# Graph layer on one NeuronCore: the ring of gathered rows and edge weights grows from eight places to twelve, and VectorE builds the weights before it adds the sums

## The chip, the cores and the metric

The kernel runs on one core of one Trainium2 chip. The metric is the device time of one execution in microseconds (us). Three runs of the kernel before took 794.12, 795.60 and 796.25 us, a median of 795.6 us.

## The reference

3125 nodes have 256 features each, and 50000 edges carry a source, a destination (sorted) and one of eight relations. Cut to the part that the change touches:

```python
xn = _layernorm(x)
W = jnp.einsum('rb,bio->rio', comp, basis)         # 8 relations out of 4 bases
h_all = jnp.einsum('ni,rio->nro', xn, W)
msgs = h_all[src, edge_types]
agg = jax.ops.segment_sum(msgs, dst, num_segments=3125)
h = gelu(agg + xn @ loop_w + h_bias + xn)          # then a layer norm
x = x + layer_norm(h) + mix(xn)                    # mix: attention without positions
x = x + ffn(_layernorm(x))                         # 32 experts, one for each node by argmax
```

The kernel turns the sum around: for each base it first sums the source rows by destination, weighted by the edge's factor for that base, and multiplies by the bases afterwards.

## The kernel before, in words

**The work.** The edges lie in 392 tiles of 128 edges. Eight tiles are an octet (49 octets, `q`), two tiles a quarter (PE's `edges(q, quarter)`), four a half. For each tile GpSimd (POOL) gathers 128 rows of `xn_d` into one place of `gath` (line 534), VectorE (DVE) builds `wmat`, which for each edge holds its four base weights at the column of its destination within a window of 36 nodes (lines 1152 and 1162, one build for each half), and TensorE (PE) multiplies gathered rows by weights (line 786). The products of a quarter stand in one PSUM bank of four; DVE adds them into `acc` at an address that it reads from a table (`add_edges`, line 1189, two adds for each quarter `w`).

**What runs beside.** `edge_schedule` writes the order by hand. Octets 0 to 6 ("max") also take the largest key of each column: PE's `key_max` (line 793) in each quarter, DVE's `reduce_max` (line 1197) after each half; the third quarter's `key_max` waits for the reduction that follows the first half. Octets 7 to 19 ("sum") compute keys (lines 800 and 801), ScalarE (ACT) their exponentials (line 621), and PE the weighted sums (line 805). Octets 20 to 22 are three small steps. Octets 23 to 48 ("chain") each finish one tile of 128 nodes: PE's `early` (817) and `product` (828), ACT's gelu, DVE's `first_stats`, `second_stats` and `finish_row` (line 1234 is its last step), PE's `turn_row` (line 840) in the third quarter, which waits for `finish_row`, and `logits` (850). After the edges comes a tail with the 32 experts.

**The ring.** `gath` and `wmat` have eight places, one for each tile of an octet. POOL's gather of tile `n` waits until tile `n - 8` was multiplied (semaphore `multiplied`, which starts at 8). DVE adds the quarter's sums, builds `hit` between the two quarters of a half, and builds the weights of the same half of the next octet at the end, when all tiles of this half are multiplied:

```python
def add_edges(q, half, bases):
    for w in range(half * OCT // PAIR // 2, (half + 1) * OCT // PAIR // 2):
        v.wait_ge(multiplied, OCT * q + PAIR * (w + 1) + OCT)
        ...
        if w % 2 == 0:
            build_hit(q + 1, half)
    build_weights(q + 1, half)
```

**The tail.** After the last octet POOL gathers 25 tiles of rows ordered by expert (line 559), PE turns them (1015) and multiplies them by the experts' weights (`hidden`, line 1025), and ACT copies and activates (718 and 729).

Of the kernel before, what the change touches and what calls it, by code (L numbers as in the profile page):

```python
# [22 lines left out]
P = 128  # L23
N, D, E = 3125, 256, 50000
R, B, X, H = 8, 4, 32, 64
KD = D // P
NT = -(-N // P)
LAST = N - (NT - 1) * P
NPAD = NT * P
WIN = 36  # L30
PAIR = 2
OCT = 8
NOCT = -(-E // (P * OCT))
# [69 lines left out]
def gps_layer(nc, x, src_t, type_rows, dst_t, dst_rows, basis, comp, loop_w, h_bias, ln_gamma, ln_beta,  # L103
              w_qk, b_qk, w_v, b_v, bn_gamma, bn_beta, router_w, router_b, w1_t, b1_t, w2_t, relation_of,
              group_mask, out):
    with ExitStack() as ctx:
        def sb(name, shape, dt=F32):
            return ctx.enter_context(nc.sbuf_tensor(name, shape, dt))
# [18 lines left out]
        gath = sb("gath", [P, OCT, D])  # L127
        wmat = sb("wmat", [P, OCT, B, WIN])
        hit = sb("hit", [P, OCT // 2, WIN])
# [123 lines left out]
        gathered = [sem(f"gathered{k}") for k in range(OCT)]  # L253
# [67 lines left out]
        f_in = [sem(f"f_in{s}") for s in range(NT)]  # L321
# [174 lines left out]
        def _(pool):  # L496
# [34 lines left out]
            def octet(q, beside, i):  # L531
                for k in range(OCT):
                    pool.wait_ge(multiplied, OCT * q + k + 1)
                    g.indirect_dma_start(gath[:, k, :], None, xn_d,  # L534
                                         bass.IndirectOffsetOnAxis(ap=src_i[:, OCT * q + k:OCT * q + k + 1], axis=0)).then_inc(gathered[k], 16)
# [21 lines left out]
            for t in range(NT):  # L557
                n = rows(t)
                g.indirect_dma_start(token[0:n, t, 0:2 * D], None, rows_d,  # L559
                                     bass.IndirectOffsetOnAxis(ap=inv_i[0:n, t:t + 1], axis=0)).then_inc(f_in[t], 16)  # L560
# [176 lines left out]
        def _(pe):  # L737
# [38 lines left out]
            def edges(q, quarter):  # L776
                if quarter % 2 == 0:
                    pe.wait_ge(wmat_built, 2 * q + quarter // 2 + 1)
                pair = range(PAIR * quarter, PAIR * quarter + PAIR)

                pe.wait_ge(added, KD * (4 * q + quarter + 1))
                for m in range(KD):
                    for k in pair:
                        if m == 0:
                            pe.wait_ge(gathered[k], 16 * q + 16)
                        ins = t_.matmul(ps_edge[quarter][:, m * B * WIN:(m + 1) * B * WIN], gath[:, k, m * P:(m + 1) * P],  # L786
                                        wmat[:, k, :, :].rearrange("p b w -> p (b w)"), start=k == pair[0], stop=k == pair[-1])
                        if m == KD - 1:
                            ins.then_inc(multiplied, 1)
# [196 lines left out]
            def rank_and_experts():  # L986
# [90 lines left out]
        def _(v):  # L1077
# [68 lines left out]
            def build_hit(q, half):  # L1146
# [4 lines left out]
                v.wait_ge(wmat_built, n) if not isinstance(q, int) or n > 0 else None  # L1151
                d.tensor_tensor(hit[:, :, :], rel[:, cut].unsqueeze(2).to_broadcast([P, w, WIN]),
                                iota[:, 0:WIN].unsqueeze(1).to_broadcast([P, w, WIN]), ALU.is_equal).then_inc(hit_built, 1)

            def build_weights(q, half):
                w = OCT // 2
                n = 2 * q + half
                cut = ds(OCT * q + half * w, w) if not isinstance(q, int) else slice(OCT * q + half * w, OCT * q + half * w + w)
# [3 lines left out]
                d.tensor_tensor(wmat[:, half * w:half * w + w, :, :], hit[:, :, :].unsqueeze(2).to_broadcast([P, w, B, WIN]),  # L1162
                                wts[:, :, cut].rearrange("p b t -> p t b").unsqueeze(3).to_broadcast([P, w, B, WIN]),
                                ALU.mult).then_inc(wmat_built, 1)

            for half in range(2):
                build_hit(0, half)
                build_weights(0, half)
# [212 lines left out]
            def rank_and_experts(o):  # L1381
# [87 lines left out]
                def finish(t):  # L1469
                    n = rows(t)  # L1470
                    place = f_ys[0:n, t * D:(t + 1) * D]
                    v.wait_ge(f_in[t], 16)
# [109 lines left out]
```

## Time and profile before

| | |
|---|---|
| median of 3 runs | 795.6 us (794.12 to 796.25) |
| the profiled execution's own time | 790.61 us |
| its span, first to last instruction | 788.7 us |
| mean granted TensorE clock | 0.886 |
| busy: PE, POOL, DVE, ACT | 585.8, 458.2, 386.3, 163.5 us |
| first edge product to the last | 53.3 to 631 us |

Busy time says how long an engine executed, not what set the pace. "Idle before" is the time in which an engine stood still before an instruction, and the name behind it is who ended that. "remote" is a signal whose sender the profile could not match. A matmul's end in these rows is modelled, not observed.

### The profile page before, as it was taken

Reading aid. Unit: us, or ns where it says so; the run is one execution under the profiler, and the core shown is the slowest. Engines: PE = TensorE matmul, PEld = TensorE weight load, DVE = VectorE, ACT = ScalarE, POOL = GpSimd, SP = SyncE. Lnnn points to the kernel's source line nnn. Section 1 sums busy time; section 2 is a strip of 40 time slices with the busy share of each in tenths; the row PEclk is TensorE's granted clock in tenths of the full one; section 3 lists DMA queues with packets and bytes.
Section 4 is the critical chain, followed back from the end, with each engine's and each line's share of the span. In section 5 each row is a group of like instructions: output and inputs, shape, how many; then the busy total and the mean of one; then the engine's idle time right before and its main releaser. Section 6 shows DMA issues by size and latency. Waiting matters only on the chain.

```text
span 788.7 us, 10440 instructions
## 1 busy us (share of the span) xinstructions
PE 585.8 (74%) x3181; PEld 471.6 (60%) x3181; DVE 386.3 (49%) x1272; ACT 163.5 (21%) x345; POOL 458.2 (58%) x464
## 2 busy tenths in 40 slices
PE   0366686888888768698999798897979982419980
PEld 0356675666665647477777666775858741318860
DVE  2844445333322334446666646456547677303552
ACT  0450000000000001022332312132122350115520
POOL 9146676666666666566676667666666400740165
PEclk9969999898999998699999888899989995559986
DMA  8563333333333344234434433334334326640021
GB/s 227 157 185 88 87 99 88 90 89 91 93 91 94 91 141 121 68 94 126 123 115 131 126 112 115 103 114 128 110 108 130 108 99 166 200 126 2 15 81 72
DMA packets 41872, 86.78 MB, mean 110 GB/s; under 512 B 11280, under 2 KB 23378, under 8 KB 41491
## 3 DMA queue, kind: packets, MB, share of 16 engines
q0 software_dynamic: 22576, 61.01, 26.7%
q1 hardware_dynamic: 18372, 22.95, 9.4%
q10 hardware_dynamic: 864, 2.08, 1.1%
q8 instruction: 29, 0.48, 0.2%
q14 instruction: 31, 0.25, 0.1%
HBM read 73.21 MB, written 12.80 MB: 109 GB/s over the span
## 4 chain that ended last, share of the span: by engine, by line
PE 56%; another core or an unknown queue 14%; DVE 10%; issue 7%; DMA 4%; POOL 3%; ACT 2%; SPq 1%; DVEq 0%; ACTq 0%; POOLq 0%
PE ps L786 23%; PE ps L828 11%; PE ps L817 6%; PE ps L1025 3%; PE ps L1034 2%; PE ps L793 2%; DMA both<-in_x 2%; PE ps L800 2%; POOL gath L534 2%; PE ps L805 2%; DMA gath<-xn_d,src_i 1%; POOL out L564 1%; PE ps L850 1%; PE ps L840 1%
## 5 line engine op out<-in xcount | busy, mean ns | idle before, releaser
L534 POOL DMA_INDIRECT gath<-xn_d,src_i x392 | 386.5, 986 | 214.9 <-issue 90.9
L786 PE MATMUL ps<-wmat,gath 128*128 128x144 f32 x1568 | 257.8, 309 | 25.5 <-DMA gath<-xn_d,src_i 10.7
L786 PEld LDWEIGHTS ps<-wmat,gath 128*128 128x128 f32 x1568 | 229.4, 203 | 50.8 <-issue 22.4
L1189 DVE TENSOR_TENSOR acc_raw<-acc_raw,ps 128x144 f32 x392 | 101.8, 300 | 283.2 <-PE ps L786 203.5
L1162 DVE TENSOR_TENSOR wmat<-hit,wts 128x576 f32<-128x576 f32 x100 | 75.3, 753 | 0.3
L564 POOL DMA_INDIRECT out<-acc_raw,inv_i x25 | 25.4, 1015 | 55.5 <-DVE acc_raw L1473 49.1
L1482 DVE SCALAR_TENSOR_TENSOR acc_raw<-ps,wts,acc_raw 128x256 f32 x56 | 27.0, 482 | 59.7 <-PE ps L1034 46.6
L559 POOL DMA_INDIRECT both<-rows_d,inv_i x25 | 24.3, 971 | 52.6 <-DVE inv_i L1436 45.2
L828 PE MATMUL ps<-wk_et,acc_raw 128*128 128x256 f32 (+1 forms) x200 | 53.1, 391 | 0.0
L828 PE MATMUL ps<-wq_wv,acc_raw 128*128 128x256 f32 (+1 forms) x200 | 52.6, 388 | 0.0
L817 PE MATMUL ps<-cmat,both 128*128 128x512 f32 (+1 forms) x100 | 52.5, 651 | 0.0
L1025 PE MATMUL ps<-acc_raw,gath 128*64 x224 | 33.3, 308 | 24.9 <-ACT acc_raw L718 22.7
L1025 PEld LDWEIGHTS ps<-acc_raw,gath 128*64 128x64 f32 x224 | 28.8, 156 | 30.7 <-issue 30.7
L793 PE MATMUL ps<-both,wk_et 128*128 128x256 f32 (+1 forms) x104 | 29.9, 414 | 18.4 <-DVE top L1197 18.4
L828 PEld LDWEIGHTS ps<-wq_wv,acc_raw 128*128 128x128 f32 (+1 forms) x200 | 36.9, 193 | 4.8 <-issue 0.2
L805 PE MATMUL ps<-both,wk_et 128*128 128x257 f32 (+1 forms) x100 | 28.5, 410 | 14.8 <-ACT wk_et L621 7.8
L828 PEld LDWEIGHTS ps<-wk_et,acc_raw 128*128 128x128 f32 (+1 forms) x200 | 35.1, 194 | 3.6 <-issue 0.2
L621 ACT ACTIVATE wk_et<-ps 128x256 f32<-128x256 f32 x24 | 9.2, 384 | 126.9 <-remote 71.3
L840 PE MATMUL ps<-ident,both 128*128 128x128 f32 (+1 forms) x50 | 11.2, 308 | 31.4 <-issue 16.4
L750 PE MATMUL ps<-ident,both 128*128 128x128 f32 x50 | 10.8, 387 | 31.6 <-DVEq L1116 23.7
L793 PEld LDWEIGHTS ps<-both,wk_et 128*128 128x128 f32 x104 | 19.6, 210 | 21.8 <-DVE top L1197 19.6
L646 ACT ACT_TABLE_LOAD x25 | 32.1, 1283 | 0.5
(194 smaller groups left out, 619.7 us busy)
## 6 DMA issues: line engine op xcount, KB each, us to landing
gath<-xn_d,src_i POOLq DMA_INDIRECT x392
rows_d<-both SPq DMA_DIRECT2D x24, 256.0 KB
both<-in_x SPq DMA_DIRECT2D x24, 128.0 KB
both<-in_x SPq DMA_DIRECT2D x4, 640.0 KB, 17.2
xn_d<-both SPq DMA_DIRECT2D x4, 640.0 KB
acc_raw<-in_w_t SPq DMA_DIRECT2D x1, 2080.0 KB
acc_raw<-in_w_t SPq DMA_DIRECT2D x1, 2048.0 KB, 7.5
acc_raw<-in_type_rows ACTq DMA_DIRECT2D x1, 1600.0 KB, 15.6
```

What stands on the lines that cost most here:

```text
L534: g.indirect_dma_start(gath[:, k, :], None, xn_d, bass.IndirectOffsetOnAxis(ap=src_i[:, OCT * q + k:OCT * q + k + 1], axis=0)).then_inc(ga ...
L564: g.indirect_dma_start(out, bass.IndirectOffsetOnAxis(ap=inv_i[0:n, t:t + 1], axis=0), f_ys[0:n, t * D:(t + 1) * D], None).then_inc(f_stor ...
L646: s.activation(h[0:n, t % 2, :], ps_mix[t % 2][0:n, 0:D], ACT.Gelu).then_inc(c.gelu_done, 1)
L786: ins = t_.matmul(ps_edge[quarter][:, m * B * WIN:(m + 1) * B * WIN], gath[:, k, m * P:(m + 1) * P], wmat[:, k, :, :].rearrange("p b w -> ...
L793: ins = t_.matmul(ps_mix[m][:, 0:n], wk[:, k, m * P:(m + 1) * P], xnt[:, k, ds(first, n)], start=k == 0, stop=k == KD - 1)
L805: ins = t_.matmul(ps_sum[m][:, 0:D + 1], et[0:n, j, m * P:(m + 1) * P], tile, start=start, stop=stop)
L817: t_.matmul(bank, xnt[:, k, P * t:P * t + n], cmat[:, k, :], start=k == 0, stop=False)
L828: ins = t_.matmul(ps_mix[t % 2][0:n, 0:D], acc[:, f, t * P:t * P + n], basis_sb[m][:, b, :], start=False, stop=f == KD * B - 1, skip_group ...
L1025: ins = t_.matmul(ps[4 + g % 2][0:H, f * P:(f + 1) * P], f_w[:, g % 2, f, k * H:(k + 1) * H], xts[:, ds(tiles[f] * D + k * P, P)], start=k ...
L1162: d.tensor_tensor(wmat[:, half * w:half * w + w, :, :], hit[:, :, :].unsqueeze(2).to_broadcast([P, w, B, WIN]), wts[:, :, cut].rearrange(" ...
L1189: d.tensor_tensor(place, place, ps_edge[w][:, m * B * WIN:(m + 1) * B * WIN].rearrange("p (b w) -> p b w", w=WIN), ALU.add).then_inc(added, 1)
L1482: d.scalar_tensor_tensor(place, ps[g % 2 * 2 + f // 2][:, f % 2 * D:(f % 2 + 1) * D], limit[:, p:p + 1], place, ALU.min, ALU.max).then_inc ...
```

## The change

`gath` and `wmat` now have `SLOTS = 12` places, three halves of four. Tile `n` uses place `n % 12`. The gather of tile `n` waits for the product of tile `n - 12`. The weights of half `2q + half + 2` are built at the start of `add_edges(q, half)`, ahead of its adds, and wait for the products of half `2q + half - 1`. Besides, in the tail two tiles share one `f_in` semaphore, so PE and DVE wait for two gathers where they waited for one.

```diff
+HALF = OCT // 2
+SLOTS = 3 * HALF
-        gath = sb("gath", [P, OCT, D])
-        wmat = sb("wmat", [P, OCT, B, WIN])
-        hit = sb("hit", [P, OCT // 2, WIN])
+        gath = sb("gath", [P, SLOTS, D])
+        wmat = sb("wmat", [P, SLOTS, B, WIN])
+        hit = sb("hit", [P, HALF, WIN])
...
-                for k in range(OCT):
-                    pool.wait_ge(multiplied, OCT * q + k + 1)
-                    g.indirect_dma_start(gath[:, k, :], None, xn_d,
-                                         bass.IndirectOffsetOnAxis(ap=src_i[:, OCT * q + k:OCT * q + k + 1], axis=0)).then_inc(gathered[k], 16)
+                for n in range(OCT * q, OCT * q + OCT):
+                    pool.wait_ge(multiplied, OCT + max(n - SLOTS + 1, 0))
+                    g.indirect_dma_start(gath[:, n % SLOTS, :], None, xn_d,
+                                         bass.IndirectOffsetOnAxis(ap=src_i[:, n:n + 1], axis=0)).then_inc(gathered[n % SLOTS], 16)
...
-                        pe.wait_ge(f_in[t], 16)
+                        if t % 2 == 0:
+                            pe.wait_ge(f_in[t // 2], 16 * min(2, NT - t))
...
-            def build_weights(q, half):
-                w = OCT // 2
-                n = 2 * q + half
-                cut = ds(OCT * q + half * w, w) if not isinstance(q, int) else slice(OCT * q + half * w, OCT * q + half * w + w)
-                if not isinstance(q, int) or q > 0:
-                    v.wait_ge(multiplied, OCT * q + half * w + w)
+            def build_weights(n):
+
+                cut = slice(HALF * n, HALF * n + HALF)
+                at = n % 3 * HALF
+                if n >= 3:
+                    v.wait_ge(multiplied, OCT + HALF * (n - 2))
                 v.wait_ge(hit_built, n + 1)
...
             def add_edges(q, half, bases):
 
+                build_hit(2 * q + half + 2)
+                build_weights(2 * q + half + 2)
                 for w in range(half * OCT // PAIR // 2, (half + 1) * OCT // PAIR // 2):
                     v.wait_ge(multiplied, OCT * q + PAIR * (w + 1) + OCT)
...
-                    if w % 2 == 0:
-                        build_hit(q + 1, half)
-                build_weights(q + 1, half)
```

On VectorE, the second half of a "max" octet, before (L1189 are the adds, L1152 and L1162 the builds, L1197 the reductions):

```order
L1189 ISA [waits added,multiplied]
L1189 TENSOR_TENSOR acc_raw<-acc_raw,ps 128x4x36
L1189 ISA [waits added]
L1189 TENSOR_TENSOR acc_raw<-acc_raw,ps 128x4x36
L1152 TENSOR_TENSOR hit<-rel,iota 128x144 [waits wmat_built]
L1189 ISA [waits added,multiplied]
L1189 TENSOR_TENSOR acc_raw<-acc_raw,ps 128x4x36
L1189 ISA [waits added]
L1189 TENSOR_TENSOR acc_raw<-acc_raw,ps 128x4x36
L1162 TENSOR_TENSOR wmat<-hit,wts 128x576 [waits hit_built,multiplied]
L1197 TENSOR_REDUCE top<-ps 128x1 [waits max_mult] x2
```

The same place now:

```order
L1154 TENSOR_TENSOR hit<-rel,iota 128x144 [waits wmat_built]
L1164 TENSOR_TENSOR wmat<-hit,wts 128x576 [waits hit_built,multiplied]
L1193 ISA [waits added,multiplied]
L1193 TENSOR_TENSOR acc_raw<-acc_raw,ps 128x4x36
L1193 ISA [waits added]
L1193 TENSOR_TENSOR acc_raw<-acc_raw,ps 128x4x36
L1193 ISA [waits added,multiplied]
L1193 TENSOR_TENSOR acc_raw<-acc_raw,ps 128x4x36
L1193 ISA [waits added]
L1193 TENSOR_TENSOR acc_raw<-acc_raw,ps 128x4x36
L1198 TENSOR_REDUCE top<-ps 128x1 [waits max_mult] x2
```

Both builds moved ahead of the half's first add, and nothing stands between the last add and the reduction.

On VectorE at the end of a chain octet's first half, before (L1232 and L1234 are `finish_row`):

```order
L426 TENSOR_LOAD base_row
L1189 ISA [waits added,multiplied]
...
L1189 TENSOR_TENSOR acc_raw<-acc_raw,ps 128x4x36
L1162 TENSOR_TENSOR wmat<-hit,wts 128x576 [waits hit_built,multiplied]
L1232 RECIPROCAL both<-both 128x1 [waits once_var_b,once_std_b]
L1234 TENSOR_SCALAR both<-both 128x256 [waits v_own]
```

and now:

```order
L428 TENSOR_LOAD base_row
L1154 TENSOR_TENSOR hit<-rel,iota 128x144 [waits wmat_built]
L1164 TENSOR_TENSOR wmat<-hit,wts 128x576 [waits hit_built,multiplied]
L1193 ISA [waits added,multiplied]
...
L1193 TENSOR_TENSOR acc_raw<-acc_raw,ps 128x4x36
L1233 RECIPROCAL both<-both 128x1 [waits once_var_b,once_std_b]
L1235 TENSOR_SCALAR both<-both 128x256 [waits v_own]
```

The builds moved from between the adds and `finish_row` to between the load of the addresses and the first add. No engine has more or fewer instructions than before in the edges' part.

## Rows read from the trace of the kernel before

**Rows 1.** The page's part 1: busy us of each engine, share, instructions.
```profile
PE 585.8 (74%) x3181; PEld 471.6 (60%) x3181; DVE 386.3 (49%) x1272; ACT 163.5 (21%) x345; POOL 458.2 (58%) x464
```

**Rows 2.** Busy time in stretches: octets 0-6, 7-19, 20-22, 23-48.
```profile
core 0: us, PE busy (x) PEld busy (x) DVE busy (x) ACT busy (x) POOL busy (x), PEclk, DMA share, GB/s
53.30:135.20 81.90, 58.52 (x330) 52.88 (x330) 35.62 (x120) 0.98 (x1) 53.79 (x57) 0.92 0.32 91
135.20:283.40 148.20, 121.72 (x644) 96.70 (x643) 49.48 (x159) 9.60 (x25) 100.82 (x103) 0.94 0.32 91
283.40:325.90 42.50, 26.70 (x135) 22.02 (x133) 19.55 (x69) 4.52 (x6) 28.69 (x30) 0.76 0.42 128
325.90:631.00 305.10, 272.72 (x1456) 217.46 (x1457) 179.55 (x648) 82.88 (x129) 198.75 (x200) 0.94 0.39 114
```

**Rows 3.** Page part 5: group | busy us, mean ns | idle before, releaser.
```profile
L534 POOL DMA_INDIRECT gath<-xn_d,src_i x392 | 386.5, 986 | 214.9 <-issue 90.9
L1189 DVE TENSOR_TENSOR acc_raw<-acc_raw,ps 128x144 f32 x392 | 101.8, 300 | 283.2 <-PE ps L786 203.5
L1162 DVE TENSOR_TENSOR wmat<-hit,wts 128x576 f32<-128x576 f32 x100 | 75.3, 753 | 0.3
```

**Rows 4.** Line 534 on POOL: ns min/median/max, and its waits (us, times).
```profile
L534 POOL DMA_INDIRECT gath<-xn_d,src_i x392: 941/947/1524, 47.6 to 623.6; - x196
...
  issue: 90.9, 297
  PE ps L786: 70.0, 73
  remote: 29.5, 21
```

**Rows 5.** Timeline in octets 2 and 3: start us, us, engine line, [idle before <-releaser].
```profile
80.06 1.14 PE L786 MATMUL ps<-wmat,gath 128*128 128x144 f32 x8
...
82.53 0.95 POOL L534 DMA_INDIRECT gath<-xn_d,src_i  x1 [0.30 <-issue]
85.34 0.52 DVE L1189 TENSOR_TENSOR acc_raw<-acc_raw,ps 128x144 f32 x2 [3.57 <-remote]
85.43 0.95 POOL L534 DMA_INDIRECT gath<-xn_d,src_i  x1 [1.95 <-remote]
85.77 0.75 DVE L1162 TENSOR_TENSOR wmat<-hit,wts 128x576 f32<-128x576 f32 x1
86.44 0.75 DVE L1197 TENSOR_REDUCE top<-ps 128x1 f32<-128x256 f32 x2
...
86.92 1.72 PE L793 MATMUL ps<-both,wk_et 128*128 128x256 f32 x4 [3.87 <-DVE top L1197]
```

**Rows 6.** Waits of PE, octets 0 to 6: us in total, times, longest us.
```profile
PE ps L793 <- DVE top L1197: 18.4, 6, 3.9
```

**Rows 7.** Waits of PE and then of POOL, octets 7 to 22.
```profile
PE ps L786 <- DMA gath<-xn_d,src_i: 9.9, 14, 1.6
...
POOL gath L534 <- PE ps L786: 18.2, 23, 2.4
POOL gath L534 <- remote: 12.0, 9, 2.1
```

**Rows 8.** Waits of PE, octets 23 to 48.
```profile
PE ps L840 <- issue: 16.4, 12, 5.4
PE ps L840 <- DVE both L1234: 12.3, 4, 4.1
```

**Rows 9.** Busy time in octets 37 and 46 (columns as in rows 2).
```profile
488.00:505.40 17.40, 15.12 (x62) 11.47 (x61) 6.79 (x25) 2.34 (x5) 11.81 (x13) 0.74 0.42 122
...
599.10:609.90 10.80, 10.69 (x62) 8.56 (x61) 8.10 (x30) 3.91 (x6) 7.19 (x8) 1.00 0.41 123
```

**Rows 10.** Timeline in the tail, while POOL gathers 25 tiles (672 to 701 us).
```profile
679.03 3.67 PE L1025 MATMUL ps<-acc_raw,gath 128*64 x16 [1.11 <-ACT acc_raw L718]
...
697.28 1.12 ACT L729 ACTIVATE gath<-ps,acc_raw 64x128 f32<-64x128 f32 x4 [18.40 <-remote]
```

More of the change, by code:

```diff
@@ L251, in gps_layer @@
         loopw_ready = sem("loopw_ready")
-        gathered = [sem(f"gathered{k}") for k in range(OCT)]
+        gathered = [sem(f"gathered{k}") for k in range(SLOTS)]
         multiplied = sem("multiplied")
@@ L320, in gps_layer @@
         w2_loaded = sem("w2_loaded")
-        f_in = [sem(f"f_in{s}") for s in range(NT)]
+        f_in = [sem(f"f_in{j}") for j in range(PAIRS + 1)]
         f_turned = sem("f_turned")
@@ L559, in _ @@
                 g.indirect_dma_start(token[0:n, t, 0:2 * D], None, rows_d,
-                                     bass.IndirectOffsetOnAxis(ap=inv_i[0:n, t:t + 1], axis=0)).then_inc(f_in[t], 16)
+                                     bass.IndirectOffsetOnAxis(ap=inv_i[0:n, t:t + 1], axis=0)).then_inc(f_in[t // 2], 16)
             for t in range(NT):
@@ L778, in edges @@
                     pe.wait_ge(wmat_built, 2 * q + quarter // 2 + 1)
-                pair = range(PAIR * quarter, PAIR * quarter + PAIR)
+                pair = range(OCT * q + PAIR * quarter, OCT * q + PAIR * quarter + PAIR)
                 pe.wait_ge(added, KD * (4 * q + quarter + 1))
                 for m in range(KD):
-                    for k in pair:
+                    for n in pair:
                         if m == 0:
-                            pe.wait_ge(gathered[k], 16 * q + 16)
-                        ins = t_.matmul(ps_edge[quarter][:, m * B * WIN:(m + 1) * B * WIN], gath[:, k, m * P:(m + 1) * P],
-                                        wmat[:, k, :, :].rearrange("p b w -> p (b w)"), start=k == pair[0], stop=k == pair[-1])
+                            pe.wait_ge(gathered[n % SLOTS], 16 * (n // SLOTS) + 16)
+                        ins = t_.matmul(ps_edge[quarter][:, m * B * WIN:(m + 1) * B * WIN], gath[:, n % SLOTS, m * P:(m + 1) * P],
+                                        wmat[:, n % SLOTS, :, :].rearrange("p b w -> p (b w)"), start=n == pair[0], stop=n == pair[-1])
                         if m == KD - 1:
@@ L1144, in _ @@
             v.wait_ge(wts_ready, -(-TC // CB))
-            def build_hit(q, half):
-                w = OCT // 2
-                n = 2 * q + half
-                cut = ds(OCT * q + half * w, w) if not isinstance(q, int) else slice(OCT * q + half * w, OCT * q + half * w + w)
-                v.wait_ge(wmat_built, n) if not isinstance(q, int) or n > 0 else None
-                d.tensor_tensor(hit[:, :, :], rel[:, cut].unsqueeze(2).to_broadcast([P, w, WIN]),
-                                iota[:, 0:WIN].unsqueeze(1).to_broadcast([P, w, WIN]), ALU.is_equal).then_inc(hit_built, 1)
@@ L1155, in build_weights, with build_hit @@
-            def build_weights(q, half):
-                w = OCT // 2
-                n = 2 * q + half
-                cut = ds(OCT * q + half * w, w) if not isinstance(q, int) else slice(OCT * q + half * w, OCT * q + half * w + w)
-                if not isinstance(q, int) or q > 0:
-                    v.wait_ge(multiplied, OCT * q + half * w + w)
+            def build_hit(n):
+                cut = slice(HALF * n, HALF * n + HALF)
+                if n > 0:
+                    v.wait_ge(wmat_built, n)
+                d.tensor_tensor(hit[:, :, :], rel[:, cut].unsqueeze(2).to_broadcast([P, HALF, WIN]),
+                                iota[:, 0:WIN].unsqueeze(1).to_broadcast([P, HALF, WIN]), ALU.is_equal).then_inc(hit_built, 1)
@@ L1161, in build_weights @@
+            def build_weights(n):
+                cut = slice(HALF * n, HALF * n + HALF)
+                at = n % 3 * HALF
+                if n >= 3:
+                    v.wait_ge(multiplied, OCT + HALF * (n - 2))
                 v.wait_ge(hit_built, n + 1)
-                d.tensor_tensor(wmat[:, half * w:half * w + w, :, :], hit[:, :, :].unsqueeze(2).to_broadcast([P, w, B, WIN]),
-                                wts[:, :, cut].rearrange("p b t -> p t b").unsqueeze(3).to_broadcast([P, w, B, WIN]),
+                d.tensor_tensor(wmat[:, at:at + HALF, :, :], hit[:, :, :].unsqueeze(2).to_broadcast([P, HALF, B, WIN]),
+                                wts[:, :, cut].rearrange("p b t -> p t b").unsqueeze(3).to_broadcast([P, HALF, B, WIN]),
@@ L1164, in build_weights @@
                                 ALU.mult).then_inc(wmat_built, 1)
             for half in range(2):
-                build_hit(0, half)
-                build_weights(0, half)
+                build_hit(half)
+                build_weights(half)
             d.memset(acc_raw[:, 0:TC * P].bitcast(BF16), 0.0).then_inc(acc_zeroed, 1)
@@ L1471, in finish @@
                     place = f_ys[0:n, t * D:(t + 1) * D]
-                    v.wait_ge(f_in[t], 16)
+                    v.wait_ge(f_in[t // 2], 16 * min(2, NT - t // 2 * 2))
                     d.tensor_tensor(place, place, token[0:n, t, D:2 * D], ALU.add).then_inc(f_rows, 1)
```

## The prediction

> **What bounds the kernel now.** I read the engines' busy time first. PE is busy for 585.8 of 788.7 us and POOL for 458.2 [rows 1], so neither is full and a wait must set the pace. The stretches tell where: octets 0 to 6 take 81.9 us or 11.7 each, 7 to 19 take 148.2 or 11.4 each, 20 to 22 take 42.5, and the 26 chain octets 305.1 or 11.7 each [rows 2]. Three kinds of work at one pace is the first thing to see.
>
> POOL's own limit comes next. A gather takes 0.986 us on average, and behind it stands an issue gap of 90.9 / 297 = 0.31 us, so eight cost 10.3 us and, at the median of 0.947 us, 10.0 us [rows 3, 4]. Over this POOL stood for 70.0 + 29.5 us in 94 waits, 70.4 us without the gap that each would have anyway: that is what a ring that never blocks could give POOL [rows 4]. DVE has much room: 283.2 us of idle time before its adds [rows 3].
>
> The timeline of octets 2 and 3 shows how they hang together. PE's second quarter ends at 81.2, but DVE's add that waits for it starts at 85.34 and POOL's next gather at 85.43; then the weights are built (85.77), the reduction follows (86.44), and only then PE goes on (86.92), after 3.87 us of standing still [rows 5]. So two things lie in series with PE: a product's signal that comes 4.1 us behind the modelled end of the product, and 0.67 us (85.77 to 86.44) of building ahead of the step that PE wants.
>
> The Trainium skill's Perfetto Trace Analysis (Tensor Engine Instruction) says that a matmul's reported end is computed and that the signal follows only when PSUM has acknowledged the writes; it gives no duration for that, and 4.1 us is the row's.
>
> **The change, part by part.**
>
> *Weights ahead of the adds.* The same 98 builds run, at 0.753 us, and as many of `hit`; none is added or removed. They move into idle time: DVE waits for products before most adds. What follows a half's last add comes 0.67 us sooner, if DVE was waiting for that add's product; if DVE came late itself, nothing changes, since both builds then stand ahead of the add instead of behind it. In octets 0 to 6, PE waits six times, 18.4 us in all, for the reduction [rows 6]: 6 x 0.67 = 4.0 us off. In the chain PE waits 12 + 4 = 16 times, 28.7 us in all, at `turn_row`, which follows `finish_row` [rows 8]: 16 x 0.67 = 10.7 us off. Bounds for both: 0 below (another wait ends last), and all of the 18.4 and 28.7 us above. What is queued behind a build is the first add of the half, up to 1.05 us later; its bank is wanted again an octet later, so I take nothing. The build's own wait is for the products of the half before the present one, whose sums were already added, so it never holds DVE.
>
> *Twelve places instead of eight.* No gather is added, and none is cheaper. In octets 7 to 22 PE waits for a gather 14 times, 9.9 us in all, and POOL stood for 18.2 + 12.0 us in 32 waits, 20.4 us over its usual gap [rows 7]. Four places more let POOL go on through these. I take half of PE's waits, 5 us, because in the octets where PE waits for rows POOL had often just been streaming without a pause. Bounds: 0, and POOL's 20.4 us. In the chain, rows are not what PE waits for (its waits are at line 840), so I take nothing there.
>
> *Clock.* Octet 37 has the instructions of octet 46 but kept PE busy for 15.12 against 10.69 us, at a granted clock of 0.74 against 1.00, which means stretches at 1.2 instead of 2.4 GHz; it follows an octet where PE stood still [rows 9]. Fewer stops should give some of this back. I take 0; the bound is four such octets, 4 x 4.4 = 18 us.
>
> *Two tiles for one `f_in`.* The first expert products want four turned tiles anyway, so the later wait is covered by that. Without the cover it costs a gather's pace once, 1.3 us. I take 0.
>
> **The sum:** 4.0 + 10.7 + 5 = 19.7 us off the profiled execution's 790.6 us gives 770.9 us. The median of the runs stands 5.0 us above that execution, so the forecast is **776 us**. By the bounds alone it could lie between 797 and 710 us.
>
> **The rivals.**
>
> *No change: POOL's pause is what lets the signals through.* In rows 5 everything is silent from 83.5 us on, and the late signals come only after POOL has stopped. In the tail it is plainer: PE's `hidden` ends at 682.7 us, POOL gathers on until 701 us, and ACT gets `hidden`'s signal 18.4 us after it began to wait [rows 10]. If products' signals get through mainly when gathers pause, POOL's cycle is eight gathers and one pause: 8 x 1.25 + 1.65 = 11.65 us, which is the pace seen. Then a bigger ring only moves the pause, since it too fills up, and DVE's earlier reduction meets nobody in need of it. Against it: other adds start 0.1 us after their product while POOL works. Time 795.6 us, 790 to 799.
>
> *Slower: the longer stream holds signals longer.* Same rows, one step on. A ring of twelve lets POOL run four gathers, 4 x 1.25 = 5.0 us, further before it stops. Where PE waits for something that hangs on its own signals (the 16 waits at line 840, the six at 793), the wait grows by up to 5.0 us and shrinks by 0.67. If the four longest of the chain take all of it, they add 20 us, and the other 18 waits give back 12: 8 us slower, 804 us; if all 22 do, 95 us. It decides as soon as the mean extra hold passes 0.67 us per wait.
>
> *Much faster: POOL was the limit.* If signals are late only because POOL is at its ring's end, each octet falls to POOL's 10.3 us or, in the chain, to the 10.8 us of octet 46 [rows 9]: 7 x 10.3 against 81.9, 16 x 10.3 against 190.7, 26 x 10.8 against 305.1, in all 60 us off, 735 us. For it: 70 us of POOL's waits. Against it: PE waits for rows in 14 cases only. This case has a price of its own. A gather took up to 1.524 us where the median is 0.947, and all of them 386.5 - 392 x 0.947 = 15 us too long [rows 3, 4]; if each of the 98 builds met a gather and cost it 0.58 us, POOL would lose 57 us instead, 42 more, and this case would end at 777 us. The number of builds is the same as before, so I keep today's share.
>
> The Trainium skill's SBUF — State Buffer (SBUF: two separate sides) says that VectorE with two SBUF inputs and a GpSimd operation that reads SBUF exclude each other for a whole instruction. By that each build could hold a gather for 0.75 us, 98 x 0.75 = 74 us if each met one; the trace shows the longer gathers, at most 0.58 us over the median.
>
> **How the numbers follow.** A measurement of this kernel can tell about 0.3% from no change, 2.4 us. The forecast's case gets 0.46 (nearly all of it faster), no change 0.21 (a fifth of it faster, the rest same or slower), slower 0.20 (a little of it still faster), much faster 0.13. That makes faster 0.62, same 0.15, slower 0.23. The range runs from 750, which leaves out the lower half of the much faster case, to 806, which leaves out the upper part of the slower one. The forecast's own range is 765 to 788 us.
>
> **What would show it.** Right: the reduction and `finish_row` start directly behind the second add, PE's waits at lines 793 and 840 shrink to about 14 and 18 us, and POOL's waits in octets 7 to 22 fall below 10 us. The first case of no change: the octets keep 11.4 to 11.7 us and POOL still pauses once in each. Slower: longer waits of DVE before its adds, and more octets at a low clock. Wrong altogether would be an edge stretch that grows while PE waits at places that are not in these rows.

## Result and profile after

The changed kernel took 801.68 us (median of 4 runs, 800.66 to 802.71), the kernel before 795.13 in the same set (794.12 to 796.25). The ratio is 1.0082, with a 95% interval of 1.006 to 1.0104: slower by 0.8%, where I had forecast 776 us and faster. The range held it. Three more sets, on three chips, gave 1.0061 (1.0034 to 1.0088), 1.0032 (1.0015 to 1.0049) and 1.0069 (1.0045 to 1.0093). The profiled execution took 802.71 us, with a span of 800.9 against 788.7.

Part 1 of the page of the changed kernel, busy us of each engine:

```profile
PE 593.8 (74%) x3180; PEld 479.9 (60%) x3181; DVE 399.7 (50%) x1272; ACT 164.0 (20%) x345; POOL 457.6 (57%) x464
```

No engine has more instructions (one matmul record is missing), yet PE is busy 8.0 us longer than in [rows 1]: the same matmuls at a lower granted clock, 0.863 instead of 0.886 on average.

The same four stretches of octets as in [rows 2], changed kernel (columns as there):

```profile
53.10:136.00 82.90, 58.37 (x330) 51.31 (x330) 37.34 (x120) 0.92 (x1) 54.19 (x57) 0.92 0.32 91
136.00:291.40 155.40, 124.16 (x643) 100.63 (x642) 54.68 (x159) 9.58 (x25) 102.92 (x106) 0.89 0.31 90
291.40:335.10 43.70, 28.96 (x134) 24.73 (x134) 19.56 (x68) 4.52 (x6) 28.93 (x30) 0.69 0.42 125
335.10:642.40 307.30, 275.86 (x1452) 220.44 (x1453) 184.73 (x644) 83.41 (x129) 195.75 (x196) 0.92 0.38 111
```

Against [rows 2] they grow by 1.0, 7.2, 1.2 and 2.2 us, 11.6 of the span's 12.2. Per octet the pace is what it was, 11.8 in the first stretch and 11.8 in the chain. So nothing became slower all along. The loss must sit in single places, and which ones one profile can't say (6.2 of the 7.2 us of octets 7 to 19 are octet 7, below). The next view is of POOL.

POOL's waits at the gathers (line 536 now; what [rows 4] showed for line 534), then their group in part 5 (as [rows 3]):

```profile
  issue: 89.9, 293
  PE ps L788: 70.4, 68
  remote: 35.8, 30
```

```profile
L536 POOL DMA_INDIRECT gath<-xn_d,src_i x392 | 386.3, 985 | 220.4 <-issue 89.9
```

The larger ring didn't remove POOL's waiting: 106.2 us in 98 waits, where 99.5 in 94 stood before. Its timeline tells why. Changed kernel, octet 2 and the start of octet 3 (the places of [rows 5], which all lie in octet 2):

```profile
80.54 1.14 PE L788 MATMUL ps<-wmat,gath 128*128 128x144 f32 x8
82.08 1.03 DVE L1193 TENSOR_TENSOR acc_raw<-acc_raw,ps 128x144 f32 x4 [1.49 <-PE ps L788]
82.17 0.94 POOL L536 DMA_INDIRECT gath<-xn_d,src_i  x1 [1.93 <-PE ps L788]
83.03 0.75 DVE L1198 TENSOR_REDUCE top<-ps 128x1 f32<-128x256 f32 x2
...
88.10 0.52 DVE L1193 TENSOR_TENSOR acc_raw<-acc_raw,ps 128x144 f32 x2 [2.81 <-PE ps L788]
...
93.93 0.94 POOL L536 DMA_INDIRECT gath<-xn_d,src_i  x1 [2.00 <-PE ps L788]
```

POOL still pauses once in eight gathers (82.17 and 93.93 are 11.76 us apart: 8 x 1.25 and a pause), although its rows now lie 7 to 13 us ahead of PE (2 to 9 before). Two quarters' adds run back to back at the pause (x4 at 82.08). What PE waits for at lines 795 and 842 (793 and 840 before), octets 0 to 6 and then the chain:

```profile
PE ps L795 <- issue: 15.7, 8, 7.6
PE ps L795 <- DVE top L1198: 8.2, 7, 1.8
...
PE ps L842 <- issue: 8.8, 3, 5.0
PE ps L852 <- issue: 7.0, 4, 2.4
PE ps L842 <- DVE both L1235: 6.5, 2, 3.6
PE ps L788 <- DVE bias L1347: 6.3, 1, 6.3
PE ps L842 <- DVE acc_raw L1193: 5.6, 4, 2.2
```

Line 795 grew from 18.4 [rows 6] to 23.9 us, with one wait of 7.6 in octet 0. Line 842 fell from 28.7 [rows 8] to 20.9, but lines 852 and 788 took 16.7, where the same two (850 and 786) took 7.7 before.

One place shows the mechanism bare. Changed kernel, octet 7: PE makes the first keys (lines 802 and 803), and ACT waits for them (line 631):

```profile
140.36 0.29 PE L803 MATMUL ps<-shift,onesb 3*53 3x256 bf16 x1
...
149.10 0.95 POOL L536 DMA_INDIRECT gath<-xn_d,src_i  x1 [0.30 <-issue]
...
152.48 0.38 ACT L631 ACTIVATE wk_et<-ps 53x256 f32<-53x256 f32 x1 [98.45 <-remote]
152.70 1.03 DVE L1193 TENSOR_TENSOR acc_raw<-acc_raw,ps 128x144 f32 x4 [2.78 <-remote]
152.79 0.95 POOL L536 DMA_INDIRECT gath<-xn_d,src_i  x1 [2.74 <-remote]
152.91 2.08 PE L807 MATMUL ps<-both,wk_et 53*128 53x257 f32 x4 [10.02 <-ACT wk_et L631]
```

The keys end at 140.65 by the record. ACT, DVE and POOL all hear from PE within 0.3 us of each other at 152.5, 2.4 us after POOL's last gather ended. PE stands still for 10.02 us, since ACT's answer is what it needs. (The size of this one is chance: octet 7 took 18.9 us here, but 8.3, 10.3 and 9.8 us in three more profiles of the same kernel.)

### The profile page after: what moved, and what is told of

It reads as the page before. It is cut to its first block, busy times and chain, and to the rows that moved or that the text cites. A ratio compares the mean times of both kernels' runs of the same rounds, so it can differ in the third digit from the quotient of the medians.

```text
span 800.9 us, 10429 instructions
## 1 busy us (share of the span) xinstructions
PE 593.8 (74%) x3180; PEld 479.9 (60%) x3181; DVE 399.7 (50%) x1272; ACT 164.0 (20%) x345; POOL 457.6 (57%) x464
## 4 chain that ended last, share of the span: by engine, by line
PE 50%; another core or an unknown queue 26%; DVE 8%; issue 6%; ACT 3%; DMA 3%; SPq 1%; POOL 1%; DVEq 0%; POOLq 0%; ACTq 0%
PE ps L788 19%; PE ps L830 10%; PE ps L819 6%; PE ps L1028 3%; PE ps L1037 3%; PE ps L807 2%; DMA both<-in_x 2%; PE ps L802 2%; PE ps L852 1%; PE ps L842 1%; DVE acc_raw L1193 1%; PE ps L820 1%; DVE stats L1103 1%; PE ps L1018 1%
## 5 line engine op out<-in xcount | busy, mean ns | idle before, releaser
L788 PEld LDWEIGHTS ps<-wmat,gath 128*128 128x128 f32 x1568 | 232.3, 206 | 41.8 <-issue 25.6
L819 PE MATMUL ps<-cmat,both 128*128 128x512 f32 (+1 forms) x100 | 55.5, 684 | 0.0
L795 PE MATMUL ps<-both,wk_et 128*128 128x256 f32 (+1 forms) x104 | 30.2, 416 | 23.9 <-issue 15.7
L807 PE MATMUL ps<-both,wk_et 128*128 128x257 f32 (+1 forms) x100 | 31.6, 445 | 21.0 <-ACT wk_et L631 10.0
L807 PEld LDWEIGHTS ps<-both,wk_et 128*128 128x128 f32 (+1 forms) x100 | 19.6, 216 | 26.3 <-ACT wk_et L631 10.2
L1154 DVE TENSOR_TENSOR hit<-rel,iota 128x144 f32<-128x144 f32 x100 | 30.5, 305 | 9.4 <-issue 5.5
```

Of the source, the lines that this page charges most:

```text
L795: ins = t_.matmul(ps_mix[m][:, 0:n], wk[:, k, m * P:(m + 1) * P], xnt[:, k, ds(first, n)], start=k == 0, stop=k == KD - 1)
L807: ins = t_.matmul(ps_sum[m][:, 0:D + 1], et[0:n, j, m * P:(m + 1) * P], tile, start=start, stop=stop)
L819: t_.matmul(bank, xnt[:, k, P * t:P * t + n], cmat[:, k, :], start=k == 0, stop=False)
```

## The experiments

**Theory H:** on this chip PE's signals are held while POOL streams gathers and get through when it pauses; a larger ring lengthens the stream, so that a signal is held longer. **Rival O:** the new order on DVE costs the time. **Rival L:** the signals are late for PE's own reasons, whatever POOL does. My runs fell on four chips. On three, the kernel before took 790.6 and 800.2 (one chip, twice), 791.0 and 798.7 us; on the fourth 693.2. Where an expectation names a time in us, it was set against 795.6 us; on the chip of e1 to e4 the kernel before took 790.55, so I compare ratios. e6, e7, e8, e10 and e11 are one execution each.

### The two halves of the change

`e1_order_alone` keeps the order (and the twelve places) and takes the longer lead from the gathers:

```diff
-                    pool.wait_ge(multiplied, OCT + max(n - SLOTS + 1, 0))
+                    pool.wait_ge(multiplied, n + 1)
```

> The changed kernel with one thing undone: the gather of tile n waits for the product of tile n-8 again; twelve places of weights and the builds ahead of the adds stay. Theory H (PE's signals are held while POOL streams gathers, so a longer stream before POOL's pause costs where somebody waits): 793 to 797 us, octet 7 back from 18.9 to about 13 us, pace still 11.4 to 11.7 us per octet. Rival O (the new order on DVE costs the time, since PE's products now wait for adds behind builds): 801 us or more, octet 7 may stay long. Rival of the forecast (the order alone brings 14 us): 781 us.

Measured: 788.93 against 790.55 us, ratio 0.9973 (0.9951 to 0.9995).

`e2_ring_alone` keeps the ring and takes back the order:

```diff
-                build_hit(2 * q + half + 2)
-                build_weights(2 * q + half + 2)
...
+                    if w % 2 == 0:
+                        build_hit(2 * q + half + 2)
+                build_weights(2 * q + half + 2)
```

> The changed kernel with the other thing undone: DVE builds hit between the two quarters and the weights after the half's adds, as before, for the same half as the change (two halves ahead); the ring of twelve stays for gathers and weights. Theory H: 800 to 804 us, since the longer stream alone costs it; octet 7 18 to 19 us. Rival O (the order costs it): 794 to 796 us.

Measured: 797.2 us, ratio 1.0062 (1.0029 to 1.0095). So O falls. The order gains a quarter of a per cent, and the ring alone costs 0.6%, what the changed kernel costs on the same chip (1.0061, below). A second measurement of the order alone, `e12_order_alone_again`, on another chip:

> The changed kernel with the gathers' wait for tile n - 8 again (as e1). Where before takes about 693 us: the same time as the changed kernel within 0.5%, since POOL is not stopped by either ring; ratio 0.99 to 1.005. Where before takes about 790 us: 0.995 to 1.000, some 0.8% below the changed kernel.

Measured: 788.69 against 790.95 us, ratio 0.9974 (0.9956 to 0.9993), beside 1.0032 for the changed kernel on that chip.

Where the ring costs is seen in the stretches of the two halves (columns as in [rows 2]). Octets 0 to 6 and 20 to 22, the order alone:

```profile
53.40:133.80 80.40, 59.26 (x330) 53.78 (x331) 37.59 (x120) 0.93 (x1) 53.05 (x56) 0.89 0.32 92
285.30:324.80 39.50, 23.28 (x135) 20.53 (x134) 19.41 (x68) 4.52 (x6) 26.10 (x27) 0.81 0.41 123
```

the ring alone:

```profile
53.60:141.00 87.40, 56.22 (x330) 50.27 (x330) 35.65 (x120) 0.97 (x1) 58.94 (x61) 0.92 0.32 92
291.30:331.60 40.30, 23.02 (x134) 20.37 (x132) 19.01 (x66) 4.52 (x6) 27.29 (x28) 0.79 0.42 125
```

Their spans differ by 9.5 us (796.2 and 786.7), octets 0 to 6 by 7.0, octets 20 to 22 by 0.8. All profiles but those of the fourth chip agree. With the lead of twelve (seven profiles: this kernel, the changed one four times, e3 and e4) octets 0 to 6 took 82.9 to 87.4 us, with the lead of eight (six: the kernel before three times, e1, e12 and e9) 79.1 to 81.9, on average 5.5 us less. Octets 20 to 22 took 38.7 to 43.7 against 38.7 to 42.5, and the ranges of octets 7 to 19 and of the chain overlap as well.

Octet 22, a chain of small steps, misleads here: the order alone and then the ring alone,

```profile
308.80:324.80 16.00, 8.15 (x56) 6.79 (x54) 10.01 (x39) 2.16 (x3) 11.11 (x12) 0.85 0.33 94
311.00:331.60 20.60, 9.67 (x55) 7.83 (x53) 10.64 (x40) 2.17 (x3) 13.48 (x15) 0.75 0.36 105
```

It took 20.6 to 24.2 us in six of the seven profiles with the longer lead (17.1 in e3) and 15.9 to 19.1 in the others. But octets 20 and 21 together took 3.8 us less with the ring alone (19.7 and 23.5), so most of its extra time is only moved.

In octet 0 the cost can be followed. Changed kernel:

```profile
54.98 1.14 PE L788 MATMUL ps<-wmat,gath 128*128 128x144 f32 x8
...
64.64 0.52 DVE L1193 TENSOR_TENSOR acc_raw<-acc_raw,ps 128x144 f32 x2 [8.27 <-remote]
...
70.48 0.94 POOL L536 DMA_INDIRECT gath<-xn_d,src_i  x1 [3.17 <-PE ps L788]
```

and the order alone:

```profile
56.83 1.27 PE L788 MATMUL ps<-wmat,gath 128*128 128x144 f32 x8
61.38 0.52 DVE L1193 TENSOR_TENSOR acc_raw<-acc_raw,ps 128x144 f32 x2 [4.71 <-PE ps L788]
61.47 0.94 POOL L536 DMA_INDIRECT gath<-xn_d,src_i  x1 [1.36 <-PE ps L788]
```

With the lead of eight POOL first pauses after 10 gathers (in all six profiles), with the lead of twelve after 16 or 17 (in all seven). The add comes 3.3 us behind the modelled end of its product in the order alone and 8.5 us in the changed kernel. Octet 0 took 13.4 to 18.5 us with the longer lead and 11.7 to 15.0 with the shorter. Later on the streams are no longer than before (POOL still pauses once in eight gathers), and why octets 1 to 6 lose some 3 us more isn't shown.

### Pauses put where a signal is wanted

`e3_pause_octet7` adds one wait to the changed kernel:

```diff
+                    if n == 67:
+                        pool.wait_ge(keyed, 1)
```

> The changed kernel with one added wait: POOL's gather of tile 67 (it started at 144.10 us) waits for the keys of the last node tile, whose matmul PE ended at 140.65 us and whose signal ACT got at 152.48. Theory H: POOL pauses from 143.8 on and the signal arrives 2 to 3 us after that, near 146 us; octet 7 takes 12 to 14 instead of 18.9 us and the kernel 795 to 797 us, although a wait was added. Rival L (the signal is late for reasons of PE's own, whatever POOL does): ACT still gets it near 152 us, POOL stands still for 8 us more, 801 to 809 us.

Measured: 795.09 us, ratio 1.0055 (1.0036 to 1.0073). Its octet 7 (PE's line 805 is the keys, ACT's 633 their user, POOL's 538 the gathers):

```profile
143.10 0.29 PE L805 MATMUL ps<-shift,onesb 3*53 3x256 bf16 x1
...
145.09 0.38 ACT L633 ACTIVATE wk_et<-ps 53x256 f32<-53x256 f32 x1 [90.67 <-remote]
...
145.81 0.94 POOL L538 DMA_INDIRECT gath<-xn_d,src_i  x1 [1.47 <-PE ps L790]
```

The signal now came 1.7 us after the modelled end instead of 11.8, and the octet took 7.9 us instead of 18.9. The added wait stopped POOL for 1.47 us ahead of gather 67 (145.81). But this run shows nothing for H by itself: three gathers earlier POOL had made one of its own pauses (1.62 us, at 140.78), octet 7 took as little without an added wait (7.9 us with the ring alone, 8.3 to 10.3 in three profiles of the changed kernel), and octet 10 took 19.6 us. Beside 1.0061 for the changed kernel on this chip (below) no net gain can be told.

`e4_pause_tail` is the clean case, since in the tail POOL never pauses by itself:

```diff
             for t in range(NT):
                 n = rows(t)
+                if t % 4 == 1 and t > 8:
+                    pool.wait_ge(f_hid, t // 4 - 1)
                 g.indirect_dma_start(token[0:n, t, 0:2 * D], None, rows_d,
```

> The changed kernel with waits added in the tail alone: POOL's gathers of tiles 9, 13, 17 and 21 wait for the first, second, third and fourth result of PE's hidden. Theory H: ACT's 16.64 us of waiting for the first hidden falls to about 4, PE's 20.79 us before the second hidden to about 5; POOL's gathers end some 7 us later, the groups of experts go at about 7 us each until then, and the kernel takes 790 to 796 us. Rival L (late for PE's own reasons, or because the rows of later tiles are needed): ACT's wait stays above 14 us and the kernel takes 801 to 815 us.

Measured: 783.28 against 790.55 us, ratio 0.9901 (0.9864 to 0.9938), a larger gain than expected: beside the changed kernel's 1.0061 on this chip it is 1.6%. The changed kernel in the tail, as [rows 10] for the one before (line 1028 is `hidden`, 731 its user, 561 the gathers):

```profile
691.48 3.67 PE L1028 MATMUL ps<-acc_raw,gath 128*64 x16 [1.11 <-issue]
...
707.97 1.12 ACT L731 ACTIVATE gath<-ps,acc_raw 64x128 f32<-64x128 f32 x4 [16.64 <-remote]
...
711.87 1.57 POOL L561 DMA_INDIRECT both<-rows_d,inv_i  x1 [0.30 <-issue]
...
717.84 3.41 PE L1028 MATMUL ps<-acc_raw,gath 128*64 x16 [20.79 <-ACT acc_raw L720]
```

and with the pauses (lines 1030, 733, 563):

```profile
683.70 3.67 PE L1030 MATMUL ps<-acc_raw,gath 128*64 x16 [1.11 <-issue]
...
687.51 1.12 ACT L733 ACTIVATE gath<-ps,acc_raw 64x128 f32<-64x128 f32 x4 [3.96 <-PE ps L1030]
687.65 0.94 POOL L563 DMA_INDIRECT both<-rows_d,inv_i  x1 [2.59 <-PE ps L1030]
...
689.90 1.96 PE L1030 MATMUL ps<-acc_raw,gath 128*64 x16 [0.83 <-ACT acc_raw L722]
```

A wait was added to POOL and nothing else; ACT's wait fell from 16.64 to 3.96 us, PE's from 20.79 to 0.83, and from the first `hidden` to the span's end it took 97.6 instead of 109.4 us. Measured from the modelled end of the first `hidden`, ACT started after 0.14 us, in e4 and in e9 (below), the two kernels with these pauses; in the twelve other profiles in which POOL gathers the edges too, those of the fourth chip left out, it was 11.3 to 19.4 us. L falls: PE's signals are late because POOL gathers.

### What in POOL's work it is

`e6_spaced_gathers` (and `e11_spaced_gathers_again`) put a small operation ahead of each gather, so that gathers start 1.33 us apart instead of 1.25:

```diff
                     pool.wait_ge(multiplied, OCT + max(n - SLOTS + 1, 0))
+                    g.memset(inv_i[:, 0:1], 0).then_inc(paced, 1)
+                    pool.wait_ge(paced, n + 1)
```

> The changed kernel with one small memset on POOL ahead of every gather of the edges, and a wait for it, so that gathers start further apart (estimate 1.4 to 1.5 us instead of 1.25). Theory H in its plain form (only a pause with no gather in flight lets PE's signals through): the adds stay 4 to 6 us behind PE, POOL's own time rises by 1.2 to 2 us an octet, and the kernel takes 850 us or more. Theory H with a threshold (a slower stream lets signals through): the lag of the adds falls to 1 to 2.5 us, POOL needs no pause, the octet takes 11.2 to 12 us, the kernel 785 to 810 us.

> The same kernel as e6: a small memset on POOL and a wait for it ahead of each gather. Where before takes about 790 us: H in its plain form 850 us or more (each octet needs its pause besides the wider spacing); H with a threshold 730 to 790 us, since a slower stream lets signals through, with adds within 2.5 us of PE's end. Where before takes about 693 us: 727 us again, POOL's rate alone.

Measured: 727.47 us on the fourth chip, where the kernel before took 693.15, and 805.61 where it took 800.17 and the changed kernel 805.11. Both forms of H missed. The signals were not let through (DVE's longest wait for an add in octets 0 to 6 was 5.9 us), but the wider spacing was not paid for either: POOL waited 43.4 us for products instead of 110.2 in the changed kernel on this chip, so its longer work took the place of much of its pausing. So the hold is not absolute in a stream, and a longer stream does not always cost: here POOL gathered up to 22 times without a pause. In the timelines an add does start now and then while POOL gathers on, 8.3 us after DVE began to wait in octet 0 (64.64 above) and 2.8 in octet 2 (88.10 above).

`e8_direct_from_pool` (and `e10_direct_from_pool_again`) leave POOL as the issuer but replace the gather by a direct DMA of 128 neighbouring rows. That leaves out the choice of rows by edge, so these kernels don't compute the layer; they serve for their times alone:

```diff
-                    g.indirect_dma_start(gath[:, n % SLOTS, :], None, xn_d,
-                                         bass.IndirectOffsetOnAxis(ap=src_i[:, n:n + 1], axis=0)).then_inc(gathered[n % SLOTS], 16)
+                    at = n % (NT - 1) * P
+                    g.dma_start(gath[:, n % SLOTS, :], xn_d[at:at + P, :]).then_inc(gathered[n % SLOTS], 16)
```

> The changed kernel with every gather of the edges replaced by a direct DMA of 128 contiguous rows from the same engine, POOL (another choice of rows, the same bytes). If what holds the signals is that POOL makes descriptors at all (H1), the lag of the adds stays at 4 to 6 us wherever POOL streams and the octets stay near 11.7 us. If it is the gather alone, with its indices (H2), the lag falls under 2.5 us and the octets to under 11 us.

> The same kernel as e8: POOL issues direct DMAs of 128 contiguous rows in the place of its gathers, the same bytes. Where before takes about 790 us, H1 (any stream of descriptors that POOL makes holds the signals) expects octets of 11 us or more and late adds, a kernel of 700 us or more; H2 (the gather alone, or its longer busy time) expects 620 to 640 us, as on the other chip. Where before takes about 693 us: 625 us again.

`e7_direct_from_sync` takes the loads of octets 0 to 17, again of neighbouring rows, to another engine (POOL and PE then leave out these tiles and wait for the new semaphores):

```diff
+            for n in range(OCT * DIRECT):
+                sp.wait_ge(multiplied, OCT + max(n - SLOTS + 1, 0))
+                at = n % (NT - 1) * P
+                sp.dma_start(gath[:, n % SLOTS, :], xn_d[at:at + P, :]).then_inc(direct[n % SLOTS // PAIR], 16)
```

> The changed kernel with the loads of octets 0 to 17 issued by SyncE as direct DMAs of 128 contiguous rows (another choice of rows, the same bytes), in the place of POOL's gathers, with the same waits for products; from octet 18 on POOL gathers as before. Theory H (it is POOL's gathers that hold PE's signals): DVE's waits before the adds of these octets fall to under 2.5 us each, octets 0 to 6 take under 9.5 us each, octet 7 under 11, and the kernel is 30 to 55 us faster. Rival L (signals late for PE's own reasons or because of the bytes written): adds still start 4 to 6 us behind PE's end, octets stay at 10.5 us or more.

Measured: e7 642.5 and e8 624.82 us on the fourth chip; e10 648.94 us where the kernel before took 800.17, over the 620 to 640 that I expected. The first 56.6 us of the edges in e10, one window:

```profile
53.40:110.00 56.60, 56.01 (x371) 51.86 (x371) 42.55 (x138) 1.72 (x3) 34.69 (x66) 1.00 0.52 154
```

DVE's longest wait before an add there is

```profile
DVE acc_raw L1193 <- PE ps L788: 11.2, 13, 1.0
```

Where the gathers are gone, PE is busy 56.0 of 56.6 us at full clock and DVE hears of a product within 1.0 us. The same window on the fourth chip reads 55.98 us of PE and 11.2, 13, 1.0 as well, so the two chips are alike without gathers: from the first edge product to the last both took 433.7 us. They differ again in the tail, where both kernels do gather, by 159.6 against 135.5 us, which is all of the 24.1 us between their spans: ACT waited 12.3 us for the first `hidden` in e10 and never over 4.5 in e8. The hold goes with the gathers. Whether it is their indices, their longer work (0.985 against 0.538 us for a direct DMA) or that POOL issues them without a pause is not told apart: in e10 PE sets the pace, and POOL waits 0.78 us for it after every second DMA. e7 was seen only on the chip that holds nothing, so for the hold it shows nothing.

### Both gains together, and the other chip

`e5_order_and_tail` is e1 with e4's waits.

> The two parts that helped, together: the builds ahead of the adds with the gathers' wait for the product of tile n - 8, and the four waits in the tail. Theory H: both savings are in different stretches and add up: a ratio to the kernel before of 0.9973 x (0.9901 / 1.0082) = 0.979, near 774 us. Rival: the edges' tail end shifts and the two share a saving; then 780 us or more.

It fell on the fourth chip: 701.79 against 693.15 us, ratio 1.0116 (1.0084 to 1.0149), a miss by its number. Its trace shows why the number doesn't carry over. POOL's waits in octets 0 to 21 there:

```profile
POOL gath L536 <- issue: 34.1, 112, 0.3
POOL gath L536 <- PE ps L790: 19.2, 63, 0.3
```

No wait is longer than the issue gap of 0.3 us. POOL never pauses, octets 3 to 5 take 10.0 us each (my floor was 10.0 to 10.3), and no add there starts more than 2.1 us after DVE began to wait. Nothing is held on that chip: ACT started 0.14 us behind the first `hidden` in all four profiles from it (e5 to e8). So the pauses had nothing to free there: POOL waited 7.0 us for results of `hidden`, and the tail took 139.7 us, 134.1 in e6 without them. The rest of the 8.6 us isn't explained, since the kernel before has no profile from this chip.

`e9_order_and_tail_again`, the same kernel where the kernel before took 800.17 us:

> The same kernel as e5: builds ahead of the adds, gathers wait for tile n - 8, four waits in the tail. Where before takes about 790 us: ratio 0.975 to 0.985, both savings. Where before takes about 693 us: 1.01 again, since there the tail's pauses cost POOL time and buy nothing.

Measured: 786.72 us, ratio 0.9818 (0.9769 to 0.9867). It beats both kernels on such a chip; on the fourth it loses to the kernel before.

The changed kernel was measured three more times, to see it on the fourth chip:

> The changed kernel itself, once more, since chips differ: one chip ran the kernel before in 790.6 us and another in 693.2 us, where e5 lost 1.2% instead of winning. Theory H with the chip as its condition: where before takes about 790 us (PE's signals are held) the ratio is 1.005 to 1.010 again; where before takes about 693 us (signals not held) POOL needs 10.0 us an octet and never waits long for a product, so a larger ring meets nobody and the ratio is 0.99 to 1.005. If the ratio were 1.006 or more on both, the hold of signals would not be the cause of the loss.

> The changed kernel again, to see it where PE's signals are not held. Where before takes about 693 us, theory H: POOL gathers without a pause at 10.0 to 10.9 us an octet in both kernels, so the ring meets nobody and only the order of DVE's work and the two-tile wait differ; ratio 0.99 to 1.005. If the loss were not from held signals it would be 1.006 or more here too. Where before takes about 790 us: 1.005 to 1.010 as before.

> The changed kernel once more, as a2: where before takes about 693 us, theory H expects a ratio of 0.99 to 1.005; 1.006 or more there would speak for another cause. Where before takes about 790 us: 1.003 to 1.010.

and the kernel before was profiled beside it:

> The kernel before itself, for its trace. Where it takes about 693 us: POOL's waits for products are under 5 us in octets 0 to 19, adds start within 2 us of PE's modelled end, ACT's wait for the first hidden in the tail is under 4 us instead of 18.4. Where it takes about 790 us: rows as in the profile shown.

> The kernel before, for its trace, as b1: where it takes about 693 us, adds start within 2 us of PE's end and POOL's waits for products are under 5 us in octets 0 to 19; where it takes about 790 us, rows as in the profile shown.

All five fell on chips that hold signals: 805.11, 794.14 and 803.69 us for the changed kernel (ratios above), 787.87 and 798.01 for the one before, whose `hidden` in the tail left PE 24.2 and 26.3 us idle as in the profile shown. So it stays open whether the changed kernel loses, gains or neither where nothing is held.

## Why the prediction was wrong

**What bounds it** was read rightly: neither PE nor POOL full, and a product's signal that comes 4 us late in series with PE. The cause of that lateness was the open question, and I gave the case in which it lies with POOL's stream 0.41 in two rivals. It does.

**Weights ahead of the adds, 4.0 + 10.7 us.** This term failed. The order alone gives 2.1 us by its ratios (0.26 and 0.27%), and not at the waits that I named: in e1 PE's waits at line 795 come to 21.0 us (18.4 before) and those at line 842 to 28.0 (28.7). The premise was that DVE waits for one add and the build stands behind it. The build did leave the path. Such a place in the order alone, at the turn to octet 4:

```profile
102.90 0.52 DVE L1193 TENSOR_TENSOR acc_raw<-acc_raw,ps 128x144 f32 x2 [3.79 <-remote]
102.99 0.94 POOL L536 DMA_INDIRECT gath<-xn_d,src_i  x1 [1.77 <-remote]
103.33 0.75 DVE L1198 TENSOR_REDUCE top<-ps 128x1 f32<-128x256 f32 x2
103.81 1.13 PE L795 MATMUL ps<-both,wk_et 128*128 128x256 f32 x4 [4.02 <-DVE top L1198]
```

The reduction starts 0.43 us after the late add, where it was 1.10 (85.34 to 86.44 [rows 5]), and so in 12 of 13 half octets; yet PE still waits 4.02 us, 3.87 before. The step that failed is that these 0.67 us come off PE's wait at every one of the 6 + 16 places. What ended last was the late signal itself, which DVE and POOL get together (102.90 and 102.99), and doing DVE's work sooner doesn't bring that forward. In the changed kernel there is less to gain still: the adds that were held often run together (82.08 to 83.03, 0.95 us), so that an earlier quarter's pair of adds, 0.5 us, stands where the build stood.

**Twelve places, 5 us off.** This is the step that gave the wrong sign. POOL's waits in octets 7 to 22 didn't fall below 10 us; over octets 7 to 22 they are 22.9 + 12.1 us in 37 waits, after 18.2 + 12.0 in 32 [rows 7]. PE no longer waits for a gather (its waits on the DMA at line 788 are gone, 9.9 us before), but those waits were not the path: PE waits for `issue` at the same line instead, 14.2 us. What I had costed at nothing is octets 0 to 6, in which PE waits for DVE's answer to its own products: there the ring costs 7.0 us between e2 and e1, 5.5 on average over all profiles. In octet 0 the longer first stream (16 gathers, not 10) holds a signal 8.5 instead of 3.3 us; for the rest of the 5.5 us the cause is argued, not shown.

**Clock, 0.** PE's 8.0 us of added busy time is this term with the other sign, inside my bound of 18 us: 2.4 us in octets 7 to 19, 2.3 in octets 20 to 22 and 3.1 in the chain (the stretches above and [rows 2]). Octet 22 alone had 2.3: it ran at a granted clock of 0.64, 0.68 before, so more of it at 1.2 instead of 2.4 GHz. I take it for a consequence of the stops; nothing was run that shows it. The two kernels' mean clocks are not apart in every profile (0.873 for both on one chip).

**`f_in`, 0.** Nothing speaks against it: the tail from the last edge product on takes 158.5 us, 157.7 before. It wasn't tried alone.

**The rivals.** *Slower* came at 801.7 where I had said 804, with a mechanism that octet 0 shows (six more gathers in front of a wanted signal, held 5.2 us longer), and half of its places: the waits at line 793 grew by 5.5 us, those at line 840 shrank. *No change* was right on the pace: the pause is still there and the octets still take 11.8 us. A likely reason, argued and not run, is that PE can be at most one octet ahead of DVE, because four PSUM banks are all it has for sums; a pause that carries the signals is needed every eight tiles however many places the ring has. *Much faster* is what the fourth chip gives for the kernel before as it stands: 693 us. That POOL is the limit there, in octets 0 to 21, is read from e5; its chain octets take 10.5 us, as they do without gathers in e8, so there it isn't POOL. I had read "against it: PE waits for rows in 14 cases only" as evidence on POOL's rate, where it only said that POOL was being stopped by late signals.

The sign of a good guess was there: the tail [rows 10] showed a wait of 18.4 us, with the signal 14.6 us behind the modelled end (682.70 to 697.28), without any ring, and I gave it less weight than the room on DVE.

The Trainium skill's Perfetto Trace Analysis (Tensor Engine Instruction) has the semaphore update follow PSUM's acknowledgement of the writes. The traces agree that the signal comes behind the modelled end. With direct DMAs DVE waits 1.0 us at most for it (e10, the window above); with gathers it came up to 19.4 us late (the tail in b2), which that rule has no term for.

## What to carry to other kernels

When a signal arrives late, ask what else was running on the chip in that time, and look for the same hold in a stage where the suspected cause runs alone: here the tail, in which two added lines of waiting took 1.6% off the changed kernel. A deeper buffer can lengthen the producer's stream (here the first one, from 10 gathers to 16); ask who waits for an answer while it runs. And before a place is named as the one that costs, add up its neighbours: octet 22 grew by 4.6 us, octets 20 and 21 shrank by 3.8. Measure on more than one chip before a mechanism is called the kernel's.

## What the hardware showed that I had not expected

- On three chips PE's signals are held while POOL gathers: up to 11.8 us behind the modelled end in the edges (140.65 to 152.48), and 12.8 in the tail (695.15 to 707.97), 11.3 to 19.4 over the profiles without pauses there. DVE's get through: in octet 2 of the changed kernel the reduction ends at 88.96 and PE starts at 89.01 in the middle of a stream. After a pause begins, the held signal came 2.4 us after the last gather in octet 7.
- On a fourth chip the same program holds nothing: 693.2 us for the kernel before, some 100 us less; signals of `hidden` take 0.14 us (e5 to e8). Nothing in the traces says what sets the chips apart.
- Direct DMAs from POOL, 0.538 us each, hold nothing on either, at the pace that PE leaves them.
